# One transformer-and-scan block on one core: the output projection taken over two tiles of 128 positions, and the MLP products placed in the slots between

## The chip, the cores and the metric

The kernel runs on one core of a Trainium2 chip, which has a matrix engine (TensorE, PE in the rows, with PEld for its weight loads), a vector engine (VectorE, DVE), a scalar engine (ScalarE, ACT), a general engine (GpSimd, POOL) and a queue that issues transfers (SyncE, SP). Each engine works through its own list of instructions in order and waits on semaphores. The metric is the device time of one execution in microseconds (us); lower is better.

## The reference

The input x is 4 x 512 x 128 in f32. The block adds four parts to it, each on a layer-normalized input: gated linear attention, a feed-forward stage, a state-space (mamba) part, and the same feed-forward stage again:

```python
x = x + gla(layernorm(x))
x = x + ffn(layernorm(x))
x = x + mamba(layernorm(x))
x = x + ffn(layernorm(x))
```

Each feed-forward stage is itself six layers of local attention (16 heads of 64, windows of 32 that see themselves and the window before) and a gated MLP, all in f32:

```python
for i in range(6):
    h = shift_tokens(x)
    q, k, v = split(h @ Wqkv[i])                  # 128 -> 3 x 1024
    q, k = rotary(l2norm(q) * qs), rotary(l2norm(k) * ks)
    x = local_attention(q, k, v) @ Wo[i] + x      # 1024 -> 128
    h = shift_tokens(x)
    a, gate = split((norm(h) * g + b) @ W1[i] + b1)   # 128 -> 2 x 341
    x = (a * gelu(gate)) @ W2[i] + b2 + x             # 341 -> 128
```

## The kernel before

The change touches only the feed-forward stage, which runs twice. Its loop has one **iteration** `it` per layer and batch element (6 x 4 = 24 per stage) and in it four **slots** `u`, one per tile of 128 positions. The work is pipelined by hand: in slot u the engines finish the attention of tile u, make the scores of tile u+1 and project tiles u+2 and u+3. The MLP takes a whole batch element (512 positions, one instruction each) and runs one iteration behind: during iteration `it` the MLP of element `it - 1` is spread over the four slots (`mlp` in the code, false only in the first iteration). The order on each engine is written out in `pe_body`, `act_body` and `dve_body`, and semaphores hold it together; nothing is scheduled automatically.

A slot of PE goes: transposes of q (`pe_qk_t`, L279), chunk 2 of the q/k/v projection (`pe_proj`, L266 to L268, three matmuls each), the output projection of the tile before (`pe_wo`, L363), transposes of k, chunk 3, an MLP product, transposes of the probabilities (`pe_probs_t`, L294), the mask and half of the scores (L306, L313), chunk 4, in two slots an MLP product, the other half of the scores, chunk 5, a wait for the banks (`pe_pv_ready`, `pe_pv_banks`), chunk 0 of the next tile, P V (`pe_pv`, L328), and chunk 1. In this text a slot is counted from the start of P V in the rows (L328) to the next one, so that what stands above as first follows P V and one projection.

The MLP's steps: in slot 0 the centre product (`pe_center`, L369) and the variance (`pe_var`, L373); ACT takes a logarithm and an exponential of it (`act_rstd`, L534, L536, written to the tile `gelu`); DVE scales (`dve_norm`, L726, L729). Then three **up** products of 128, 128 and 85 columns, each for the gate (L385) and the value (L386), with the gelu on ACT (`act_gelu`, L547, behind a table load) and the product of the two on DVE (`dve_hidden`, L735). Then the **down** product (`pe_down`, L394) and its addition to the stream (`dve_down`, L742). Before the change the up products stand in slots 1, 2 and 2, the down product in slot 3.

The output projection, the MLP products and P V share two of PSUM's eight banks, `o_ps[0]` and `o_ps[1]`. ACT empties P V into `o_t` (`act_out_t`, L486); `pe_wo` reads it and writes 128 columns of `o_ps[0]`, which DVE adds to the stream (`dve_wo`, L719 and L720, 64 partitions each); only then may an MLP product or the next P V write the banks. V goes from ACT (`act_v`, L478) through 16 small transfers per tile, issued by SP, into `v_pairs`; ACT waits for those of the tile before. POOL adds the rotated halves (L860), scales by the norms (L870), normalizes the probabilities (L835) and, once per iteration, splits a weight (L849).

## Time and profile before

| | us |
|---|---|
| median of 3 runs | 3862.81 (3855.98 to 3873.53) |
| the profiled execution | 3830.92 |
| its span in the trace | 3829.1 |
| PE busy | 3454.3 |
| DVE, ACT, POOL busy | 3008.5, 2702.0, 2718.4 |
| output projection (L363) on PE, 3072 records | 387.9 |

The span is the time from the first to the last instruction of the trace; the profiled execution has 1.8 us around it. Each f32 matmul stands in the trace as two records, so eight matmuls are 16. Records overlap in the pipeline, so the time of a group is best read from its start to the start of what follows.

### The profile page before, as it was taken

How to read it: one execution, taken by the hardware profiler on the slowest of the kernel's cores; microseconds unless marked ns; L12 is line 12 of the kernel's file. 1: busy time of each engine (PE TensorE's matmuls, PEld its weight loads, DVE VectorE, ACT ScalarE, POOL GpSimd, SP SyncE). 2: the span in 40 equal slices, each digit the busy share in tenths (PEclk: the TensorE clock that was granted, in tenths of full speed). 3: DMA queues.
4: the chain of work that ended last, by engine and by line, in shares of the span. 5: the costliest groups of instructions: out<-in, count | busy, mean ns of one | idle time of the engine just before them, and what ended most of it. 6: DMA issues, size and time to landing. Idle time of an engine off the chain costs nothing. (4 is left out here: it accounts for less than half of the span.)

```text
span 3829.1 us, 153118 instructions
## 1 busy us (share of the span) xinstructions
PE 3454.3 (90%) x62588; PEld 2453.8 (64%) x62588; DVE 3008.5 (79%) x4752; ACT 2702.0 (71%) x7080; POOL 2718.4 (71%) x3091
## 2 busy tenths in 40 slices
PE   8799999999999999985555789999999999999996
PEld 3477777777777777762111267777777777777774
DVE  7688888878788788865888778888878888888884
ACT  2477778777878787763334468787777877787874
POOL 3588787777878787850334488787778787787872
PEclk9899999999999999996888899999999999999998
DMA  1233333333333333320000033233333333333331
GB/s 41 59 74 76 78 81 72 83 74 76 83 74 83 76 77 76 80 60 16 0 0 0 18 72 78 70 87 71 80 78 74 79 76 74 83 78 72 88 71 37
DMA packets 183102, 251.36 MB, mean 66 GB/s; under 512 B 53658, under 2 KB 74782, under 8 KB 182302
## 3 DMA queue, kind: packets, MB, share of 16 engines
q1 hardware_dynamic: 182422, 241.71, 26.5%
q8 instruction: 498, 8.16, 0.9%
q14 instruction: 182, 1.49, 0.1%
HBM read 39.13 MB, written 1.05 MB: 10 GB/s over the span
## 5 line engine op out<-in xcount | busy, mean ns | idle before, releaser
L860 POOL TENSOR_TENSOR qk_rows<-rot_products 128x512 f32<-128x512 f32 x768 | 982.4, 1281 | 213.1 <-DVE rot_products L659 212.2
L659 DVE TENSOR_TENSOR rot_products<-psum,rot_scaled 128x1024 f32<-128x1024 f32 x768 | 936.5, 1219 | 150.0 <-ACT squares L470 123.3
L870 POOL TENSOR_TENSOR qk_rows<-qk_rows,rnorm 128x512 f32<-128x512 f32 x768 | 804.0, 1078 | 15.0
L266 PE MATMUL psum<-wqkv_hi,xs_hi 128*128 128x512 f32 x1152 | 556.8, 483 | 81.3 <-DVE rot_products L659 42.4
L661 DVE TENSOR_REDUCE sumsq<-squares 128x8 f32<-128x512 f32 x768 | 518.6, 675 | 0.0
L470 ACT ACTIVATE squares<-psum 128x512 f32<-128x512 f32 x768 | 488.3, 636 | 41.6 <-PE psum L268 36.7
L478 ACT ACTIVATE v_rows<-psum 128x512 f32<-128x512 f32 x384 | 228.2, 595 | 358.1 <-DMA v_pairs<-v_rows 178.8
L835 POOL TENSOR_TENSOR probs<-probs,rden 128x512 f32<-128x512 f32 x384 | 392.5, 1043 | 103.7 <-DVE rden L709 102.7
L514 ACT ACTIVATE probs<-psum,minus_row_max 128x64 f32<-128x64 f32 x1536 | 457.2, 336 | 5.7 <-DVE minus_row_max L693 5.7
L267 PE MATMUL psum<-wqkv_lo,xs_hi 128*128 128x512 f32 x1152 | 457.3, 397 | 0.8 <-issue 0.8
L328 PEld LDWEIGHTS psum<-probs_t,v_pairs 64*64 64x64 f32 x24576 | 387.7, 135 | 109.5 <-issue 108.9
L268 PE MATMUL psum<-wqkv_hi,xs_lo 128*128 128x512 f32 x1152 | 457.7, 397 | 0.0
L328 PE MATMUL psum<-probs_t,v_pairs 64*64 64x32 f32 x24576 | 415.6, 220 | 33.8 <-issue 29.6
L363 PEld LDWEIGHTS psum<-o_t,wo 128*128 128x128 f32 x3072 | 362.0, 192 | 83.9 <-ACT o_t L486 63.1
L363 PE MATMUL psum<-o_t,wo 128*128 128x128 f32 x3072 | 387.9, 279 | 24.6 <-ACT o_t L486 17.2
L279 PE MATMUL psum<-ident,qk_rows 128*128 128x128 f32 x3072 | 401.4, 274 | 0.7 <-ACT q_t L497 0.7
L279 PEld LDWEIGHTS psum<-ident,qk_rows 128*128 128x128 f32 x3072 | 356.7, 142 | 28.1 <-issue 2.1
L1394 POOL TENSOR_TENSOR mb_hc<-mb_h,mb_c 128x512 f32<-128x512 f32 x128 | 159.7, 1268 | 293.9 <-DVE mb_h L1363 281.0
L313 PEld LDWEIGHTS psum<-k_t,q_t 64*32 64x32 f32 x24576 | 269.7, 105 | 152.3 <-issue 152.1
L514 ACT ACTIVATION_READ_ACCUMULATOR probs<-psum,minus_row_max 128x1 f32 x1536 | 354.2, 231 | 0.0
L266 PEld LDWEIGHTS psum<-wqkv_hi,xs_hi 128*128 128x128 f32 x1152 | 217.9, 189 | 179.8 <-issue 104.4
L313 PE MATMUL psum<-k_t,q_t 64*32 64x64 f32 x24576 | 332.2, 224 | 0.8 <-issue 0.8
(159 smaller groups left out, 6078.8 us busy)
## 6 DMA issues: line engine op xcount, KB each, us to landing
v_pairs<-v_rows SPq DMA_DIRECT2D x3072, 64.0 KB, 2.0
wqkv_staged<-in_Wqkv SPq DMA_DIRECT2D x52, 384.0 KB, 3.5
wo<-in_Wo SPq DMA_DIRECT2D x12, 512.0 KB, 4.7
w<-in_W SPq DMA_DIRECT2D x12, 341.0 KB, 3.4
qk_scale<-in_qk_scale SPq DMA_DIRECT2D x12, 128.0 KB, 3.4
w<-in_W SPq DMA_DIRECT2D x12, 128.0 KB
rot_base<-in_rot SPq DMA_DIRECT2D x2, 512.0 KB, 3.7
out_x<-qk_rows SPq DMA_DIRECT2D x1, 1024.0 KB, 5.1
```

Source lines behind the costliest of these rows:

```text
L266: nc.tensor.matmul(proj_ps[c % 2], xh, wh, start=True, stop=False)
L268: nc.tensor.matmul(proj_ps[c % 2], xl, wh, start=False, stop=True).then_inc(S["qkv_mm"], 1)
L279: last = nc.tensor.transpose(tr_ps[g % 2][:, i * P:(i + 1) * P], m["qk"][:, u % 2, (4 * g + i) * P:(4 * g + i + 1) * P], ident[:, :])
L313: last = nc.tensor.matmul(s_ps[par][WIN * w:WIN * w + WIN, 64 * hp:64 * hp + 64], m["qt"][rows, hp, WIN * w:WIN * w + WIN], m["kt"][rows, ...
L328: last = nc.tensor.matmul(o_ps[par][64 * j:64 * j + 64, P * (hp // 2) + WIN * w:P * (hp // 2) + WIN * w + WIN], m["vp"][rows, u % TILES, w ...
L363: last = nc.tensor.matmul(o_ps[0][:, 0:P], m["wo"][:, hp, :], m["ot"][:, hp, :], start=(hp == 0), stop=(hp == HP - 1))
L470: nc.scalar.activation(m["sq"][:, c % 2, :], proj_ps[c % 2], ACT.Square).then_inc(S["sq_done"], 1)
L514: last = nc.scalar.activation(m["p"][:, hp, 1, :], s_ps[1][:, 2 * WIN * hp:2 * WIN * (hp + 1)], ACT.Exp, bias=m["mx"][:, 1, hp:hp + 1], ac ...
L659: V.tensor_tensor(m["mm"][:, c % 2, :, :].rearrange("p a (h e) -> p a h e", e=DH), ps, cos_sin, ALU.mult)\
L661: V.tensor_reduce(m["ss"][:, HC * c:HC * c + HC], m["sq"][:, c % 2, :].rearrange("p (h e) -> p h e", e=DH), AX.X, ALU.add)\
L860: G.tensor_tensor(qk[:, c * CH:(c + 1) * CH].rearrange(half, a=2, e=DH // 2), cos, sin[:, :, ::-1, :], ALU.add)\
L870: G.tensor_tensor(part, part, m["rn"][:, u % 2, HC * c:HC * c + HC].unsqueeze(2) .to_broadcast([P, HC, DH]), ALU.mult).then_inc(S["rot_don ...
```

## The change

- `pe_wo` now takes half of the element's positions, two tiles, in one go: eight matmuls of 256 columns in place of two times eight of 128. It runs in slot 2 for tiles 0 and 1 and in slot 0 of the next iteration for tiles 2 and 3. `o_t` has room for two tiles, and DVE's addition covers 256 columns in the same two slots, behind the third of the four rotations.
- The up products 0 and 1 stand in slot 1, product 2 and the down product in slot 3. The first of each pair stands where the output projection stood, the second behind chunk 4.
- ACT's gelus and DVE's `hidden` follow; `dve_down` stands behind the norm's seed in slot 3. P V in slot 1 now waits for both of slot 1's `hidden` steps, in slot 2 for nothing of the MLP, in slot 3 as before for the stream.
- The normalized input overwrites the centred one (`ln_xc`), which saves a buffer.

The core of the diff:

```diff
-            m["ot"] = fsb("o_t", [P, HP, P])
-            m["xn"] = fsb("xn_mlp", [P, T])
+            m["ot"] = fsb("o_t", [P, HP, 2, P])
+            m["xn"] = ln_xc
...
             elif u == 1:
-                nc.tensor.wait_ge(S["h_done"], 2 * e + 1)
-            elif u == 2:
-                nc.tensor.wait_ge(S["hidden_done"], e + 1)
-            else:
+                nc.tensor.wait_ge(S["h_done"], 2 * (e + 1))
+            elif u == 3:
                 nc.tensor.wait_ge(S["stream"], B + e + 1)
...
-        def pe_wo(it, u):
...
+        def pe_wo(it, half):
+
+            if half == 0:
+                nc.tensor.wait_ge(S["wo_in"], (it // B + 1) * 16)
+            nc.tensor.wait_ge(S["oT_ev"], cnt(it, 2, 2 * half + 1, 2))
             for hp in range(HP):
-                last = nc.tensor.matmul(o_ps[0][:, 0:P], m["wo"][:, hp, :], m["ot"][:, hp, :],
+                last = nc.tensor.matmul(o_ps[0][:, 0:2 * P], m["wo"][:, hp, :],
+                                        m["ot"][:, hp, :, :].rearrange("p a q -> p (a q)"),
                                         start=(hp == 0), stop=(hp == HP - 1))
...
-                if prev:
-                    pe_wo(it, u - 1)
+                if mlp and u == 0:
+                    pe_wo(it - 1, 1)
+                if u == 2:
+                    pe_wo(it, 0)
+                if mlp and u == 1:
+                    pe_up(it - 1, 0, free)
+                if mlp and u == 3:
+                    pe_up(it - 1, 2, free)
...
-                if mlp and u in (1, 2):
-                    pe_up(it - 1, u - 1, added_)
-                if mlp and u == 3:
-                    pe_down(it - 1, added_)
                 pe_probs_t(it, u, nxt)
...
-                if mlp and u == 2:
-                    pe_up(it - 1, 2, added_)
+                if mlp and u == 1:
+                    pe_up(it - 1, 1, None)
+                if mlp and u == 3:
+                    pe_down(it - 1)
...
-                if mlp and u in (1, 2):
-                    act_gelu(it - 1, u - 1)
+                if mlp and u == 1:
+                    act_gelu(it - 1, 0)
+                if mlp and u == 3:
+                    act_gelu(it - 1, 2)
                 act_probs_t(it, u)
...
-                if mlp and u == 2:
-                    act_gelu(it - 1, 2)
-                if mlp and u in (1, 2):
+                if mlp and u == 1:
+                    act_gelu(it - 1, 1)
+                if mlp and u in (1, 3):
                     nc.scalar.preload_act_table_set("natural_log_exp_and_others")
...
-                if prev:
-                    dve_wo(it, u - 1)
                 if proj:
-                    dve_rotate(layer, j, u + 2, (2, 3))
+                    dve_rotate(layer, j, u + 2, (2,))
+                if mlp and u == 0:
+                    dve_wo(it - 1, 1)
+                if u == 2:
+                    dve_wo(it, 0)
+                if proj:
+                    dve_rotate(layer, j, u + 2, (3,))
                 if mlp and u == 1:
                     dve_hidden(it - 1, 0)
-                if mlp and u == 2:
+                if mlp and u == 3:
+                    dve_hidden(it - 1, 2)
+                if proj:
+                    dve_rnorm(it, u + 2)
+                if mlp and u == 1:
                     dve_hidden(it - 1, 1)
                 if mlp and u == 3:
                     dve_down(it - 1)
-                if proj:
-                    dve_rnorm(it, u + 2)
-                if mlp and u == 2:
-                    dve_hidden(it - 1, 2)
```

`free` is the count of `o_t` writes up to the slot before, so that an up product does not write the banks before ACT has emptied P V from them. The lines after the change are numbered by one to seven higher (L279 becomes L280, L328 L329, L363 L362, L735 L742).

PE in slot 1 before: the output projection (L363), transposes of k (L279), chunk 3, the first up product (L385, L386), transposes of the probabilities (L294), mask and first half of the scores.

```order
L363 MATMUL psum<-o_t,wo 128x128 x8
L279 MATMUL psum<-ident,qk_rows 128x128 x8
L266 MATMUL psum<-wqkv_hi,xs_hi 128x512
L267 MATMUL psum<-wqkv_lo,xs_hi 128x512
L268 MATMUL psum<-wqkv_hi,xs_lo 128x512
L385 MATMUL psum<-xn_mlp,w 128x512
L386 MATMUL psum<-xn_mlp,w 128x512
L294 MATMUL psum<-ident,probs 128x128 x8
L306 MATMUL psum<-maskrow,onehot 128x512 x2
L313 MATMUL psum<-k_t,q_t 32x64 x32
```

And after, from the second half of the first up product (L387) to the first of the second:

```order
L387 MATMUL psum<-ln_xc,w 128x512
L280 MATMUL psum<-ident,qk_rows 128x128 x8
L267 MATMUL psum<-wqkv_hi,xs_hi 128x512
L268 MATMUL psum<-wqkv_lo,xs_hi 128x512
L269 MATMUL psum<-wqkv_hi,xs_lo 128x512
L295 MATMUL psum<-ident,probs 128x128 x8
L307 MATMUL psum<-maskrow,onehot 128x512 x2
L314 MATMUL psum<-k_t,q_t 32x64 x32
L267 MATMUL psum<-wqkv_hi,xs_hi 128x512
L268 MATMUL psum<-wqkv_lo,xs_hi 128x512
L269 MATMUL psum<-wqkv_hi,xs_lo 128x512
L386 MATMUL psum<-ln_xc,w 128x512
```

The output projection is gone from the slot; between the first up product and the second stand two sets of transposes, chunk 3, half of the scores and chunk 4, where there was one product in the slot.

PE in slot 3 before, from the output projection to the transposed probabilities, with the down product (L394) between:

```order
L363 MATMUL psum<-o_t,wo 128x128 x8
L279 MATMUL psum<-ident,qk_rows 128x128 x8
L266 MATMUL psum<-wqkv_hi,xs_hi 128x512
L267 MATMUL psum<-wqkv_lo,xs_hi 128x512
L268 MATMUL psum<-wqkv_hi,xs_lo 128x512
L394 MATMUL psum<-hidden,w 128x512 x3
L294 MATMUL psum<-ident,probs 128x128 x8
```

And after, from the transposed probabilities (L295) to the second half of the scores (L314):

```order
L295 MATMUL psum<-ident,probs 128x128 x8
L307 MATMUL psum<-maskrow,onehot 128x512 x2
L314 MATMUL psum<-k_t,q_t 32x64 x32
L267 MATMUL psum<-wqkv_hi,xs_hi 128x512
L268 MATMUL psum<-wqkv_lo,xs_hi 128x512
L269 MATMUL psum<-wqkv_hi,xs_lo 128x512
L394 MATMUL psum<-hidden,w 128x512 x3
L314 MATMUL psum<-k_t,q_t 32x64 x32
```

The down product moved behind the transposed probabilities, half of the scores and chunk 4, and an up product stands where the output projection stood.

DVE in slot 2 before, from the second rotation (L659 with its sum L661) over the addition (L719, L720) to hidden 1 (L735):

```order
L659 TENSOR_TENSOR rot_products<-psum,rot_scaled 128x1024
L661 TENSOR_REDUCE sumsq<-squares 128x8
L719 TENSOR_TENSOR x_ffn<-psum,x_ffn 64x128
L720 TENSOR_TENSOR x_ffn<-psum,x_ffn 64x128
L659 TENSOR_TENSOR rot_products<-psum,rot_scaled 128x1024
L661 TENSOR_REDUCE sumsq<-squares 128x8
L659 TENSOR_TENSOR rot_products<-psum,rot_scaled 128x1024
L661 TENSOR_REDUCE sumsq<-squares 128x8
L735 SCALAR_TENSOR_TENSOR hidden<-psum,layer_vectors,gelu 128x512
```

And after, rotations (L665, L667), the addition (L726, L727) and the seed of the norms (L688):

```order
L665 TENSOR_TENSOR rot_products<-psum,rot_scaled 128x1024
L667 TENSOR_REDUCE sumsq<-squares 128x8
L665 TENSOR_TENSOR rot_products<-psum,rot_scaled 128x1024
L667 TENSOR_REDUCE sumsq<-squares 128x8
L726 TENSOR_TENSOR x_ffn<-psum,x_ffn 64x256
L727 TENSOR_TENSOR x_ffn<-psum,x_ffn 64x256
L665 TENSOR_TENSOR rot_products<-psum,rot_scaled 128x1024
L667 TENSOR_REDUCE sumsq<-squares 128x8
L688 TENSOR_SCALAR minus_sumsq<-sumsq 128x32
```

The addition covers 256 columns and stands one rotation later.

## Rows read from the trace of the kernel before

A few words recur: x16 behind a row is a count of records; "[0.71 <-ACT gelu L534]" is idle time before the row and what ended it.

**Rows 1.** The page: busy time of each engine, share of the span, instructions
```profile
PE 3454.3 (90%) x62588; PEld 2453.8 (64%) x62588; DVE 3008.5 (79%) x4752; ACT 2702.0 (71%) x7080; POOL 2718.4 (71%) x3091
```

**Rows 2.** Windows: feed-forward stage, then slots 0 to 3 (length, busy per engine, clock)
```profile
core 0: us, PE busy (x) PEld busy (x) DVE busy (x) ACT busy (x) POOL busy (x), PEclk, DMA share, GB/s
400.00:1600.00 1200.00, 1163.05 (x23530) 881.33 (x23523) 978.77 (x1605) 947.94 (x2571) 962.78 (x1117) 1.00 0.33 78
1330.60:1346.72 16.12, 15.30 (x321) 11.83 (x320) 13.20 (x22) 12.82 (x38) 13.44 (x17) 1.00 0.34 75
1346.72:1362.25 15.53, 15.02 (x321) 11.70 (x320) 13.63 (x23) 13.46 (x36) 13.88 (x16) 1.00 0.40 96
1362.25:1380.05 17.80, 17.33 (x325) 12.53 (x324) 12.74 (x23) 14.93 (x38) 14.66 (x19) 1.00 0.27 62
1380.05:1396.06 16.01, 15.92 (x323) 12.08 (x323) 13.25 (x23) 10.54 (x32) 10.36 (x13) 1.00 0.29 69
```

**Rows 3.** Timeline of PE, slots 0 to 2: start, length, operation, records, [idle before]
```profile
1335.36 1.95 PE L363 MATMUL psum<-o_t,wo 128*128 128x128 f32 x16
...
1337.14 1.04 PE L279 MATMUL psum<-ident,qk_rows 128*128 128x128 f32 x8
...
1345.86 0.47 PE L266 MATMUL psum<-wqkv_hi,xs_hi 128*128 128x512 f32 x1 [0.71 <-ACT gelu L534]
...
1351.76 2.02 PE L363 MATMUL psum<-o_t,wo 128*128 128x128 f32 x16 [0.52 <-ACT o_t L486]
...
1353.62 1.04 PE L279 MATMUL psum<-ident,qk_rows 128*128 128x128 f32 x8
...
1355.19 1.02 PE L385 MATMUL psum<-xn_mlp,w 128*128 128x512 f32 x2
...
1356.05 1.02 PE L386 MATMUL psum<-xn_mlp,w 128*128 128x512 f32 x2
...
1356.90 1.04 PE L294 MATMUL psum<-ident,probs 128*128 128x128 f32 x8
...
1359.87 0.86 PE L313 MATMUL psum<-k_t,q_t 64*32 64x64 f32 x64
...
1364.06 0.89 PE L328 MATMUL psum<-probs_t,v_pairs 64*64 64x32 f32 x44 [0.34 <-issue]
...
1375.49 1.02 PE L385 MATMUL psum<-xn_mlp,w 128*85 128x512 f32 x2
...
1379.19 0.47 PE L266 MATMUL psum<-wqkv_hi,xs_hi 128*128 128x512 f32 x1
```

**Rows 4.** Timeline of ACT, slots 0 and 1
```profile
1344.22 0.60 ACT L478 ACTIVATE v_rows<-psum 128x512 f32<-128x512 f32 x1 [2.38 <-DMA v_pairs<-v_rows]
...
1356.00 1.28 ACT L547 ACT_TABLE_LOAD   x1
```

**Rows 5.** Groups by form, DVE's addition of the output projection: busy, mean ns
```profile
L720 DVE TENSOR_TENSOR x_ffn<-psum,x_ffn 64x128 f32<-64x128 f32 x192 | 56.6, 295 | 2.6
```

**Rows 6.** Timeline of DVE, slots 0, 1 and 3
```profile
1346.19 1.30 DVE L726 SCALAR_TENSOR_TENSOR xn_mlp<-ln_xc,layer_vectors,gelu 128x512 f32<-128x512 f32 x1
...
1348.59 1.21 DVE L659 TENSOR_TENSOR rot_products<-psum,rot_scaled 128x1024 f32<-128x1024 f32 x1
...
1358.02 0.75 DVE L735 SCALAR_TENSOR_TENSOR hidden<-psum,layer_vectors,gelu 128x512 f32<-128x512 f32 x1
...
1390.94 1.51 DVE L742 SCALAR_TENSOR_TENSOR x_ffn<-psum,layer_vectors,x_ffn 64x512 f32<-64x512 f32 x2
```

**Rows 7.** Timeline of POOL, end of slot 0 and slot 1
```profile
1344.89 4.68 POOL L870 TENSOR_TENSOR qk_rows<-qk_rows,rnorm 128x512 f32<-128x512 f32 x4
...
1349.53 1.84 POOL L849 TENSOR_TENSOR wqkv_lo<-wqkv_staged,wqkv_hi 128x768 fp32r<-128x768 f32 x1
...
1351.33 1.27 POOL L860 TENSOR_TENSOR qk_rows<-rot_products 128x512 f32<-128x512 f32 x1
...
1352.56 2.04 POOL L835 TENSOR_TENSOR probs<-probs,rden 128x512 f32<-128x512 f32 x2
```

52 lines of the change are left out of this document (24 added, 28 removed).

## The prediction, made before the change was timed

> **What bounds the kernel now.** I read the page first, then the windows, then the timeline of each engine over one pass through the loop. In the page, TensorE (PE) is busy 90% of the span and the next engine 79% [rows 1]; the reader is to see that only PE can be the bound on average. In the stretch from 400 to 1600 us, which is pure feed-forward stage, PE is busy 1163 of 1200 us at the full clock (2.4 GHz) while DVE, ACT and POOL have about 20% idle each [rows 2]. One iteration (one batch element, four slots of one tile each) lasts 65.46 us: slots 0 to 3 take 16.12, 15.53, 17.80 and 16.01 us in the iteration that I walk through [rows 2]. Both stages together hold 46 iterations with an MLP in them (24 each, the first without), some 3010 us of the 3829. So what the change does is 46 times what it does to these four slots.
>
> Busy PE is not free-running PE. In slot 0 it stands still for 0.71 us before a projection until ACT has taken the logarithm, and ACT itself had stood 2.38 us until the transfers of V had landed, before it could empty V and turn to the logarithm [rows 3, 4]. In slot 1 PE arrives at the output projection 0.52 us before the o_t that it reads [rows 3]. Slot 3, in which PE is busy 15.92 of 16.01 us, leaves 16.0 - 1.78 (output projection) - 2.57 (down product, six records of 0.43) = 11.6 us at most for what all slots have in common. Four of these, four output projections (7.12), centre and variance (1.72), three up products (5.16) and the down product (2.57) are 63.0 us: of 65.46 at least 2.5 are waits. The loop is tight: whatever PE does earlier must find its input earlier.
>
> **Part 1, the output projection over two tiles.** Before, 16 records over 128 columns take 1337.14 - 1335.36 = 1.78 us, 0.111 each [rows 3]. The trace has no 256-column record. Upper bound: a 512-column record takes 0.43 us (1356.05 - 1355.19 = 0.86 for two) [rows 3], half of that is 0.214, and 16 of them 3.43 us. Lower bound: as little as 128 columns, 1.78 us. 0.111 stands close to a quarter of 0.43 (0.107), so records grow with their columns; I take 3.43. Per iteration that is 4 x 1.78 = 7.12 before and 2 x 3.43 = 6.86 after: 0.26 us less, 12 us over 46 iterations. On DVE the two additions of about 0.295 us each per slot become two over 256 columns in every second slot [rows 5]; between 0.295 at 128 columns and 0.75 at 512 (two in 1.51) [rows 6] I put one at 0.43 us. That frees 0.6 us of DVE per iteration, which has 20% to spare: nothing by itself.
> The Trainium skill (TensorE: Matmul & The Clock Gate, section "Back-to-back issue gap") has a sustained spacing of about 81 ns a matmul at 128 columns and 131 at 512, far less than in proportion. The trace disagrees: 0.111 against 0.43, nearly the full factor of four [rows 3]. By the page the wide product would be nearly half as long as I say; that is the fifth case below.
>
> **Part 2, slot 0.** The projection of the previous element's last two tiles stands here: 3.43 in place of 1.78, and behind it the transposes, the centre product and everything to the scores, all 1.65 us later. The centre product wants DVE's addition, which now stands behind a third rotation. PE comes to it 1337.14 - 1330.60 + 1.65 + 1.57 = 9.8 us into the slot [rows 3]; I take the addition as done by then, and 0.5 us, one addition, as the upper bound. The late V transfer is now covered: V is wanted 1.65 us later, the logarithm is done before the last projection, and the 0.71 us wait goes with its queueing, about 0.9 us. Slot 0: 16.12 + 1.65 - 0.95 = 16.8 us.
>
> **Part 3, slot 1: two MLP up products, no output projection.** Three things come late for PE.
> First the normalization. It ran on DVE from 1346.19 to 1348.59, ahead of the first rotation of slot 1, whose result PE's next projection wants [rows 6]. Now it starts 1.56 us later (behind scores that end 1.65 later), while the slot starts only 0.7 later. PE reaches that projection 3.6 us into the slot and its product is there at 4.1: 0.5 us of wait; up to 2 in the one iteration in four in which DVE also rescales its tables.
> Second POOL. Its four multiplications (4.68 us), the weight split (1.84), one addition (1.27) and the probabilities (2.04) run in one piece from 1344.89 to 1354.60 [rows 7], and all that is now 1.4 us later: probabilities at about 8.7 us into the slot. PE had come to their transposition 1356.90 - 1346.72 = 10.2 us into the slot [rows 3]; without an output projection it comes at 8.2. About 0.45 us of wait where there were 2.3 of slack.
> Third the chain of the MLP itself. The second up product writes the banks that the first product's gelu (ACT) and hidden (DVE) read. From the second half of the q/k transposes to the end of hidden it takes 1358.02 + 0.75 - 1353.62 = 5.15 us: ACT has two copies, a square, a table load of 1.28 and the gelu in the way, DVE the last rotation [rows 3, 4, 6]. PE needs from that same point 4.5 us to the place where the second product now stands (1355.19 - 1353.62 = 1.57 for the transposes and a projection, then 1356.90 to 1359.87 = 2.97) [rows 3]. So 0.7 us are short at the least; through POOL's lag, which holds the last rotation, it is 1.0 or a little more. In slot 2 before, the product between the two places gave 1.7 us more, which is why no such wait is seen there.
> A matmul that waits holds all that stands behind it on PE: half of the scores, a projection and P V. Behind the second product, gelu, hidden and the bank wait take 1379.19 - 1375.49 = 3.70 us, as they did in slot 2 [rows 3], then 0.86 to the next slot. Slot 1: second product at 4.4 + 0.5 + 1.7 + 4.5 + 0.45 + 1.0 = 12.55, and 3.7 + 0.86: 17.1 us against 15.53.
>
> **Part 4, slot 2** loses two up products (3.43) and gains 1.65: free-running that is 17.80 - 1.78 = 16.0; and the waits behind the second product (1379.19 stands 0.3 late) and of P V (0.34) [rows 3] are mostly gone, with 0.3 left for o_t: 15.1 us.
>
> **Part 5, slot 3: the last up product early, the down product behind the first half of the scores.** It loses 1.78 of output projection and gains 1.72 of up product: no change in free time. But the down product wants the last hidden. Its chain is again the 5.15 us, PE is there after 4.5: with the semaphore 0.75 to 0.9 us short. Before, the down product had a hidden from the slot before and no wait. And P V waits for DVE to add the down product (1.51 us) [rows 6], which was long over; now it starts 2.6 us after the product begins and PE has only 1.7 us of work meanwhile (half of the scores and a projection): 0.25 us. Slot 3: 16.01 + 1.0 = 17.0 us.
>
> **The sum.** 16.8 + 17.1 + 15.1 + 17.0 = 66.0 against 65.46: 0.54 us longer, 25 us over 46 iterations. The profiled execution took 3830.92 us and would take 3856; it is 32 us under the median of the runs, 3862.81, to which I add the same 25: 3888 us.
> The same number of table loads stands on ACT (two before gelus, two back per iteration); the output projection at each stage's end is 1.65 longer, 3 us in all, against first iterations that gain as much. The transfers of V take as long and are issued in the same order. The normalized input now overwrites the centred one; that waits only on products of the element before, over by then. These I put at zero, with 5 us either way.
>
> **Rivals.** A change of 0.5%, 19 us, is about what a measurement of this kernel can tell from none.
> Case 1, as summed: 3888, between 3870 and 3910. Chance 0.42.
> Case 2, waits only move: the 3.8 us of waits stay as large and only the free 0.26 us counts: 3850. For it: the slots hand their lateness on, and what PE waits for in one it does not wait for in the next; against it: two products now stand closer behind their inputs than before. 0.20.
> Case 3, the other side: slot 0's gain is whole (16.5 us) and POOL's lag doesn't reach PE, so that the MLP waits stay at their least, 0.7 in slots 1 and 3. Slots 16.5, 16.5, 14.9, 16.7 make 64.6, 0.86 less: 3823. It decides at POOL's probabilities: if they are ready 8.2 us into slot 1, no wait is added there. Against it: that run of POOL has no gap in it [rows 7]. 0.20.
> Case 4, lag on lag: the late normalization, POOL and, one iteration in four, the tables push the last rotation by 0.75 us more in slots 1 and 3 each and it isn't made good in slot 2: 67.5 us, +94 in all, or half of that: 3910 to 3957. 0.15.
> Case 5, a 256-column record costs little more than a 128-column one: up to 1.65 us less per pair, 3.3 per iteration: 3888 - 152 = 3736 at the lower bound. 0.03.
> Faster by over 0.5%: cases 3 and 5, 0.23. Within: case 2 and a fifth of case 1, 0.28. Slower: the rest, 0.49. The range of 8 in 10 goes from 3832 (most of case 2 and the near part of case 3) to 3935.
> That the change doesn't do what it says can be left out: the order of the instructions shows 8 matmuls of 256 columns per two tiles and the products where described.
>
> **What would show it.** L362's records 0.214 apart. Slot 0 near 16.8 us with no idle time for the logarithm before its last projection; in slot 1 idle time before the second up product (0.7 to 1.1 us) put down to DVE's hidden, and some before the transposed probabilities put down to POOL; slot 2 near 15 us; in slot 3 0.8 us before the down product. I am wrong if the iteration comes out under 65 us, or if the longer waits stand elsewhere, above all before the centre product or for V's transfers.

## The result, and the profile after

The changed kernel takes 3953.05 us (median of four runs, 3943.11 to 3953.73) against 3864.4 us of the kernel before on the same chip: ratio 1.0223, 95% interval 1.0194 to 1.0252. It is slower by 2.2%, about 89 us. I had predicted 3888 and a range up to 3935, so the direction was right and the size was not: the time fell into my fourth case ("lag on lag", 67.5 us per iteration, 3910 to 3957), which I had given 0.15. The profiled execution took 3943.11 us (3830.92 before), 112 us more, of which 23.5 are only that the execution profiled before stood 33.5 us under its median and this one 10 under. Executions at a lower granted clock are left out of all ratios; there was one, of e8 below (4328 us at a clock of 0.73, where its others have 0.96).

The page's line of each engine, the feed-forward stage, and slots 0 to 3 of one iteration, which answer to [rows 1, 2]:

```profile
PE 3487.2 (88%) x61052; PEld 2382.9 (60%) x61052; DVE 3001.4 (76%) x4560; ACT 2703.5 (69%) x7080; POOL 2715.1 (69%) x3091
```
```profile
core 0: us, PE busy (x) PEld busy (x) DVE busy (x) ACT busy (x) POOL busy (x), PEclk, DMA share, GB/s
400.00:1600.00 1200.00, 1137.94 (x22324) 824.32 (x22323) 949.34 (x1490) 920.37 (x2489) 933.55 (x1084) 1.00 0.32 76
1025.79:1042.60 16.81, 16.72 (x321) 12.91 (x321) 12.70 (x21) 13.18 (x37) 10.45 (x14) 1.00 0.40 97
1042.60:1059.76 17.16, 15.72 (x310) 10.65 (x309) 14.28 (x23) 14.56 (x37) 15.61 (x17) 1.00 0.36 86
1059.76:1075.60 15.84, 15.23 (x317) 12.23 (x317) 12.68 (x21) 10.44 (x32) 10.65 (x15) 1.00 0.30 69
1075.60:1093.17 17.57, 16.53 (x312) 10.74 (x311) 13.09 (x21) 13.59 (x36) 15.55 (x19) 1.00 0.27 63
```
Every engine is less busy in the stage than before, PE too (1138 of 1200 us against 1163), at the same clock. So no work was added: waits were. (Per iteration PE is busy 0.6 us more than before, 0.948 of 67.48 us against 0.969 of 65.43; the products and their columns are the same, and the balance below, from start to start, shows no longer work in it.) Most sit in slots 1 and 3, where PE is idle 1.44 and 1.04 us; in slot 0 PE is busy 16.72 of 16.81 us.

**The balance.** A feed-forward iteration can be cut out of the trace 44 times with nothing missing, from P V's first record to P V's first record four slots on. Means of those, and what PE would need if each step took its shortest record of the trace (a common slot is 11.15 us: P V 2.00, six pieces of projection 4.70, transposes and scores 4.45; narrow output projection 1.78, wide 3.45, up product 1.72, down 2.58, centre and variance 1.81):

| us | slot 0 | slot 1 | slot 2 | slot 3 | iteration |
|---|---|---|---|---|---|
| before | 15.94 | 15.84 | 17.53 | 16.13 | 65.43 |
| of it waits | 1.20 | 1.19 | 1.16 | 0.62 | 4.2 |
| after | 16.90 | 17.38 | 15.54 | 17.66 | 67.48 |
| of it waits | 0.49 | 2.79 | 0.94 | 2.21 | 6.4 |
| my walk | 16.8 | 17.1 | 15.1 | 17.0 | 66.0 |

The free part fell by 0.22 us (predicted 0.26), and waits rose by 2.3. Over all 46 iterations, with those at a phase's end, the means are 65.18 and 67.30: 98 of the 112 us. The other 14 are the ends of the stages: the first iteration starts 1.8 us later, the piece between the two stages is 5.8 and the tail 7.0 us longer.

**Slots 1 and 3 on PE**, which answer to [rows 3]:

```profile
1030.40 3.72 PE L362 MATMUL psum<-o_t,wo 128*128 128x256 f32 x16
1033.96 1.04 PE L280 MATMUL psum<-ident,qk_rows 128*128 128x128 f32 x8
...
1051.27 1.09 PE L295 MATMUL psum<-ident,probs 128*128 128x128 f32 x8 [0.23 <-POOL probs L846]
...
1055.08 1.13 PE L386 MATMUL psum<-ln_xc,w 128*128 128x512 f32 x2 [0.72 <-DVE hidden L742]
...
1064.46 3.69 PE L362 MATMUL psum<-o_t,wo 128*128 128x256 f32 x16 [0.18 <-ACT o_t L490]
...
1073.81 0.27 PE L314 MATMUL psum<-k_t,q_t 64*32 64x64 f32 x2 [0.44 <-issue]
...
1087.53 2.82 PE L394 MATMUL psum<-hidden,w 128*128 128x512 f32 x6 [0.63 <-DVE hidden L742]
...
1092.31 0.47 PE L267 MATMUL psum<-wqkv_hi,xs_hi 128*128 128x512 f32 x1 [0.28 <-issue]
```
The wide product takes 3.56 us with its queueing, the second up product and the down product each wait for hidden, and behind the down product a projection has 0.28 us of idle time ahead of it, at the place of the wait for the addition. In the means the step that ends at the second up product is 0.85 us over its shortest, the product itself 0.19, the last two pieces 0.48: 1.5 us for the second product in slot 1, and by the same count 1.5 in slot 3. Before, the one such place, in slot 2, cost 0.5. That alone is 2.5 us more than before: this is where the time of the changed kernel stands. It does not say what would give it back; the experiments do.

**Why hidden is late**, on DVE, POOL and ACT [rows 4, 6, 7]:

```profile
1036.36 1.23 DVE L665 TENSOR_TENSOR rot_products<-psum,rot_scaled 128x1024 f32<-128x1024 f32 x1 [1.19 <-ACT squares L474]
...
1052.55 1.23 DVE L665 TENSOR_TENSOR rot_products<-psum,rot_scaled 128x1024 f32<-128x1024 f32 x1 [1.24 <-POOL qk_rows L871]
...
1054.29 0.74 DVE L742 SCALAR_TENSOR_TENSOR hidden<-psum,layer_vectors,gelu 128x512 f32<-128x512 f32 x1
```
```profile
1037.67 1.29 POOL L871 TENSOR_TENSOR qk_rows<-rot_products 128x512 f32<-128x512 f32 x1 [2.28 <-DVE rot_products L665]
...
1041.50 4.68 POOL L881 TENSOR_TENSOR qk_rows<-qk_rows,rnorm 128x512 f32<-128x512 f32 x4
...
1051.17 1.27 POOL L871 TENSOR_TENSOR qk_rows<-rot_products 128x512 f32<-128x512 f32 x1
```
```profile
1052.99 0.69 ACT L551 ACTIVATE gelu<-psum,layer_vectors 128x512 f32<-128x512 f32 x1
```
Read it backwards. Hidden (1054.29) follows DVE's last rotation (1052.55), which had waited 1.24 us for POOL's addition. POOL had run in one piece since 1041.50, and there it had started late after 2.28 us of idle time. What it idled for is DVE's last rotation of slot 0 (1036.36), and that had waited for the fourth piece of projection, which stands behind the wide product. The wide product in slot 0 thus costs something in slot 1. The gelu ended at 1053.68, only 0.6 us before hidden began: a second chain, nearly as late. In the means of slot 1 the last rotation ends 11.28 us in, the gelu 11.27, hidden begins at 11.82 and the second product at 12.62.

The view of waits, 400 to 1600 us (in total, times, longest), of before:
```profile
POOL qk_rows L860 <- DVE rot_products L659: 75.4, 138, 1.8
...
ACT v_rows L478 <- DMA v_pairs<-v_rows: 60.5, 31, 3.4
...
PE psum L266 <- ACT gelu L534: 9.7, 9, 1.6
...
DVE rot_products L659 <- POOL qk_rows L860: 3.0, 6, 0.6
```
and of after:
```profile
POOL qk_rows L871 <- DVE rot_products L665: 111.4, 68, 2.4
...
DVE rot_products L665 <- POOL qk_rows L871: 23.4, 25, 1.2
...
PEld psum L386 <- DVE hidden L742: 20.0, 18, 1.2
...
PEld psum L295 <- POOL probs L846: 13.1, 22, 0.8
...
PE psum L394 <- DVE hidden L742: 12.3, 18, 0.8
```
PE's wait for the logarithm is gone, and each of the 18 iterations in the window now has both waits for hidden.

### The profile page after: what moved, and what is told of

It is laid out like the page before. It is cut to its first block and busy times, and to the rows that moved or that the text cites. A ratio compares the mean times of both kernels' runs of the same rounds, so it can differ in the third digit from the quotient of the medians.

```text
span 3941.3 us, 149848 instructions
## 1 busy us (share of the span) xinstructions
PE 3487.2 (88%) x61052; PEld 2382.9 (60%) x61052; DVE 3001.4 (76%) x4560; ACT 2703.5 (69%) x7080; POOL 2715.1 (69%) x3091
## 5 line engine op out<-in xcount | busy, mean ns | idle before, releaser
L665 DVE TENSOR_TENSOR rot_products<-psum,rot_scaled 128x1024 f32<-128x1024 f32 x768 | 935.7, 1218 | 289.2 <-ACT squares L474 205.8
L667 DVE TENSOR_REDUCE sumsq<-squares 128x8 f32<-128x512 f32 x768 | 518.9, 676 | 0.0
L329 PEld LDWEIGHTS psum<-probs_t,v_pairs 64*64 64x64 f32 x24576 | 383.8, 135 | 100.8 <-issue 100.3
L329 PE MATMUL psum<-probs_t,v_pairs 64*64 64x32 f32 x24576 | 409.5, 220 | 27.7 <-issue 24.0
L280 PEld LDWEIGHTS psum<-ident,qk_rows 128*128 128x128 f32 x3072 | 362.5, 142 | 94.0 <-issue 54.7
L280 PE MATMUL psum<-ident,qk_rows 128*128 128x128 f32 x3072 | 403.3, 275 | 5.6 <-ACT q_t L501 5.4
L501 ACT ACTIVATE k_t<-psum 128x512 f32<-128x512 f32 x384 | 208.8, 596 | 285.1 <-PE psum L280 285.1
L314 PEld LDWEIGHTS psum<-k_t,q_t 64*32 64x32 f32 x24576 | 270.4, 105 | 181.7 <-issue 181.4
L362 PE MATMUL psum<-o_t,wo 128*128 128x256 f32 x1536 | 361.6, 390 | 17.7 <-ACT o_t L490 14.5
L314 PE MATMUL psum<-k_t,q_t 64*32 64x64 f32 x24576 | 335.1, 224 | 13.0 <-issue 12.9
L362 PEld LDWEIGHTS psum<-o_t,wo 128*128 128x128 f32 x1536 | 290.2, 193 | 89.5 <-issue 28.0
```

What stands on the lines that cost most here:

```text
L280: last = nc.tensor.transpose(tr_ps[g % 2][:, i * P:(i + 1) * P], m["qk"][:, u % 2, (4 * g + i) * P:(4 * g + i + 1) * P], ident[:, :])
L314: last = nc.tensor.matmul(s_ps[par][WIN * w:WIN * w + WIN, 64 * hp:64 * hp + 64], m["qt"][rows, hp, WIN * w:WIN * w + WIN], m["kt"][rows, ...
L329: last = nc.tensor.matmul(o_ps[par][64 * j:64 * j + 64, P * (hp // 2) + WIN * w:P * (hp // 2) + WIN * w + WIN], m["vp"][rows, u % TILES, w ...
L362: last = nc.tensor.matmul(o_ps[0][:, 0:2 * P], m["wo"][:, hp, :], m["ot"][:, hp, :, :].rearrange("p a q -> p (a q)"), start=(hp == 0), sto ...
L665: V.tensor_tensor(m["mm"][:, c % 2, :, :].rearrange("p a (h e) -> p a h e", e=DH), ps, cos_sin, ALU.mult)\
L667: V.tensor_reduce(m["ss"][:, HC * c:HC * c + HC], m["sq"][:, c % 2, :].rearrange("p (h e) -> p h e", e=DH), AX.X, ALU.add)\
```

## The experiments

Ratios are to the kernel before on the same chip, intervals 95%. Slots and iterations are means over the same 44 iterations of each profile.

| kernel | ratio | slots 0 to 3 | iteration |
|---|---|---|---|
| before | 1 | 15.94 15.84 17.53 16.13 | 65.43 |
| changed | 1.0223 | 16.90 17.38 15.54 17.66 | 67.48 |
| e1 wide only | 1.0168 | 16.85 15.38 19.56 15.48 | 67.27 |
| e2 spread only | 1.0294 | 15.83 18.00 15.24 19.04 | 68.11 |
| e3 changed, no tables | 1.0191 | 17.01 17.36 15.45 17.52 | 67.34 |
| e4 before, no tables | 0.9985 | 16.08 15.99 17.51 16.14 | 65.72 |
| e5 wide cut in two | 1.0263 | 18.07 17.10 15.29 17.38 | 67.84 |
| e6 e5, no tables | 1.0208 | 18.00 17.00 15.24 17.06 | 67.30 |
| e7 changed, 10 transfers | 1.0193 | 16.93 17.31 15.39 17.60 | 67.23 |
| e8 before, 10 transfers | 0.9842 | 15.17 15.84 17.30 16.09 | 64.40 |
| e10 last up product in slot 2 | 1.0512 | 17.65 17.37 18.01 16.43 | 69.45 |
| e11 e10, 10 transfers | 1.0403 | 17.88 17.31 17.51 16.23 | 68.93 |
| e12 e5, centre later | 1.0248 | 17.69 17.02 15.30 17.40 | 67.42 |
| e13 e10, addition earlier | 1.0233 | 17.10 17.39 18.04 15.18 | 67.71 |
| e14 e8, norm later | 0.9854 | 15.17 16.14 17.26 16.07 | 64.65 |

**e1 and e2: each half of the change alone.** The changed kernel with the MLP products at their old places (e1):
```diff
-                if mlp and u == 1:
-                    pe_up(it - 1, 0, free)
-                if mlp and u == 3:
-                    pe_up(it - 1, 2, free)
...
+                if mlp and u == 1:
+                    pe_up(it - 1, 0, free)
+                if mlp and u == 2:
+                    pe_up(it - 1, 1, None, it * HALVES + 1)
+                if mlp and u == 3:
+                    pe_down(it - 1, free)
                 pe_probs_t(it, u, nxt)
```
and the kernel before with the MLP products in their new slots, each behind the narrow output projection (e2; ACT and DVE follow):
```diff
-                if mlp and u in (1, 2):
+                if mlp and u in (1, 3):
                     pe_up(it - 1, u - 1, added_)
-                if mlp and u == 3:
-                    pe_down(it - 1, added_)
...
-                if mlp and u == 2:
-                    pe_up(it - 1, 2, added_)
+                if mlp and u == 1:
+                    pe_up(it - 1, 1, added_)
+                if mlp and u == 3:
+                    pe_down(it - 1, added_)
```

> The changed kernel with the wide output projection (slots 0 and 2), but the MLP products back where they stood before the change (up 0 in slot 1, up 1 and 2 in slot 2, down in slot 3, each behind chunk 3 or 4). My theory: the loss comes from the second MLP product of slots 1 and 3 waiting for gelu and hidden of the first, and from P V behind them; here those waits are gone, free time on PE is 0.26 us per iteration less than before, so an iteration takes 65.0 to 65.6 us (65.2 before, 67.3 after in the profiles) and the time is within 1% of the kernel before. Rival A: the wide projection costs by itself (longer records, DVE's addition behind the third rotation, POOL's lag in slot 1): then the iteration stays above 66.5 us and the time 1.5 to 2% above before.

> The kernel before (128-column output projection in every slot), with the MLP products placed as the change places them: up 0 and up 1 in slot 1, up 2 and down in slot 3, the second of each behind chunk 4; the first behind chunk 3 as before. My theory: between the first and the second product there is as much work as in slot 2 of the kernel before, so no wait for hidden; only P V in slot 3 now waits about 0.3 us for the addition of the down product: iteration 65.2 to 65.7 us, time within 0.7% of before. Rival B: that two products in slots 1 and 3 are bad in themselves (table load in slot 3, late hidden, the addition behind the seed): iteration over 66.3, time 1.5% or more over before.

Measured: 1.0168 [1.0131, 1.0205] and 1.0294 [1.0252, 1.0336]. My theory, that each part costs little by itself, fell, and both rivals held: each part alone costs 1.5% or more. Alone they add 1.84 and 2.68 us per iteration, together 2.05 and not 4.5: each covers a part of the other's cost. e1 shows a wait that I had not foreseen:
```profile
PE psum L280 <- ACT q_t L507: 34.6, 32, 1.4
```
In slots 1 and 3, with neither output projection nor product between the two halves of the transposes, PE reaches the second half before ACT has copied o_t and q_t: in the means the step ahead of it is 0.91 and 1.17 us over its shortest, against 0.22 and 0.21 before. The narrow output projection had been the cover for these copies, so taking 1.78 us out of slots 1 and 3 returned 0.46 and 0.65. In e2 it is V:
```profile
ACT v_rows L476 <- DMA v_pairs<-v_rows: 104.5, 39, 4.3
...
PE psum L266 <- ACT v_rows L476: 24.6, 18, 2.1
```
The transfers of slot 1's tile begin 0.5 us into slot 2, as before the change (0.4), and their 16 issues take 11.4 us (means), with 2.0 us from issue to landing. Slot 2, now without an MLP product, is too short for them: PE wants the next bank 12.9 us in, and ACT, which waits for the landing, has emptied it at 14.2. PE waits 1.4 us.

**e3 and e4: no table loads**, in the changed kernel and in the one before. Both leave out the gelu and keep its bias (in the kernel before the load stands at `u in (1, 2)`):
```diff
-                if mlp and u in (1, 3):
-                    nc.scalar.preload_act_table_set("natural_log_exp_and_others")
...
-ACT.Gelu,
+ACT.Identity,
```

> The changed kernel with the gelu replaced by an addition of the bias alone (Identity, no table loads in the loop; the MLP's gate isn't the reference's). It takes 1.28 us out of the chain from the first product to hidden. My theory: idle time of 0.68 us before the second up product and before the down product goes, and slot 1 and slot 3 get 0.7 to 1.1 us shorter each; the iteration takes 65.3 to 66.0 us against 67.3. Rival C: ACT isn't on the path there (POOL's lag holds the last rotation and so hidden): then slots 1 and 3 shrink by less than 0.4 us each.

> The same in the kernel before, as a control (bias alone in place of the gelu, no table loads). My theory: only slot 2 has a wait on that chain (hidden before P V, 0.3 us) and the V transfers start up to 1.3 us earlier after slots 1 and 2: iteration 0.3 to 0.8 us shorter, 64.4 to 64.9. Rival C: it gains as much as the changed kernel does.

Measured: 1.0191 [1.0143, 1.0239] and 0.9985 [0.9963, 1.0007]. Rival C held: slots 1 and 3 change by 0.02 and 0.14 us. The gelus of the first products end 1.4 and 1.5 us sooner, the last rotation in slots 1 and 3 ends where it did (11.3 and 10.6 us in), and the second products still stand 12.6 and 12.0 us in. So ACT's chain is not what holds them alone. (e4's mean has one iteration of 72.58 us in it; the medians of the 44 are 65.29 before and 65.25 in e4.)

**e5, e6, e12: the wide product cut in two**, heads 4 to 7 behind the fourth piece. With it the centre product moves behind the transposed probabilities (slot 0), and DVE's addition behind the last rotation (slots 0 and 2):
```diff
                 if mlp and u == 0:
-                    pe_wo(it - 1, 1)
+                    pe_wo(it - 1, 1, range(4))
...
                 if mlp and u == 0:
+                    pe_wo(it - 1, 1, range(4, HP))
+                if u == 2:
+                    pe_wo(it, 0, range(4, HP))
+                pe_probs_t(it, u, nxt)
+                if mlp and u == 0:
                     pe_center(it - 1)
-                pe_probs_t(it, u, nxt)
...
+                if proj:
+                    dve_rotate(layer, j, u + 2, (3,))
                 if mlp and u == 0:
                     dve_wo(it - 1, 1)
                 if u == 2:
                     dve_wo(it, 0)
-                if proj:
-                    dve_rotate(layer, j, u + 2, (3,))
```

(e5; e6 adds the edit of e3; e12 puts `pe_center` behind `pe_scores(it, u + 1, 0)`.)

> The changed kernel with one thing different: the wide output projection of slots 0 and 2 is cut in its list of eight heads. Heads 0 to 3 stay ahead of the last q/k transposes, heads 4 to 7 follow the fourth piece of the projection. The centre product and the addition to x move behind it. Same products, same columns. THEORY (chain over POOL): the whole wide product stands ahead of the fourth piece, which comes 1.65 us late; DVE's last rotation, POOL's norm multiplications and so POOL's probabilities and second addition of the next slot (1 and 3) follow 1.4 late, and PE waits there. With the split the fourth piece comes 1.7 us earlier in slots 0 and 2, POOL has no 2.3 us of idle time before its norm multiplications there, and the last rotation of slots 1 and 3 is no longer held by POOL. The wait for the probabilities in slot 1 (0.35 us) goes; of the 0.8 us before each second product only 0.1 to 0.3 goes, since the gelu chain on ACT ends almost as late. Iteration 66.4 to 67.0 us instead of 67.48: ratio to the kernel before 1.008 to 1.016. RIVAL (the wide product is what costs, wherever it stands): iteration 67.4 or more, ratio 1.02 to 1.025, with the waits at other places. SECOND RIVAL (waits of slots 1 and 3 come from POOL's work in that slot alone): POOL's idle time in slots 0 and 2 goes, the last rotation of slots 1 and 3 stays as late, ratio 1.02.

> The same split of the wide projection, and in addition the gelu is replaced by a copy with bias, with no table loads (the gelu is left out of what is computed). THEORY (two chains end together before the second product: POOL to the last rotation to hidden, and ACT's tables to gelu to hidden): the loads alone, taken from the changed kernel, gave 0.14 us per iteration; with both taken away the stall before the second products falls from 0.8 to 0.3 us or less in slots 1 and 3, and the iteration is 65.7 to 66.3 us, ratio 0.998 to 1.006. RIVAL (POOL's lag does not come from the place of the wide product): as the changed kernel without table loads, iteration 67.3, ratio 1.019.

> The split wide projection of the earlier run, with the centre product behind the first half of the scores instead of directly behind the transposed probabilities, where it had waited 0.77 us for the addition to x. THEORY: slots 1 to 3 stay at what the split gave them (17.1, 15.3, 17.4), and slot 0 loses the wait for the addition but takes one before the variance product, since two copies on ACT (1.2 us) now stand against one piece of projection (0.8): slot 0 17.2 to 17.6 us, iteration 67.0 to 67.4, ratio about 1.018. RIVAL (the gain in slots 1 to 3 came only because slot 0 was longer and gave POOL and ACT time): slots 1 to 3 return to 17.4, 15.5, 17.7 while slot 0 falls, iteration 67.5 or more.

Measured: 1.0263 [1.0231, 1.0295], 1.0208 [1.0166, 1.0249], 1.0248 [1.0198, 1.0298]: all three slower than I expected, e5 and e12 no faster than the changed kernel and e6 no faster than e3. Slots 1 to 3 of e5 are as expected: the wait for the probabilities is gone (1.15 to 0.78 us for the step), DVE's waits for POOL, 23.4 us in the changed kernel, don't appear among e5's, and slots 1 to 3 are 0.81 us shorter. In slot 0 my edit lost 1.17, in a place that I had not priced (1.0 of it at this place): the centre product waits for the addition, which now comes after the second half.
```profile
PE psum L371 <- DVE x_ffn L733: 12.7, 18, 0.7
```
e12 moved the centre product, slot 0 fell by 0.38, and slots 1 to 3 stayed (17.02, 15.30, 17.40). Slot 0 is still 0.79 longer than in the changed kernel, so for slot 1 this speaks against the rival (the gain is a gift of slot 0's length) without settling it. Slot 3's gain, 0.26 to 0.28, is clear of it: the slot ahead of it, slot 2, got the cut too and is shorter, not longer. e6's iteration (67.30) is the number of its rival, but not its mechanism: against e3 slots 1 to 3 gain 1.03 us and slot 0 loses 0.99. The wait before the second up product over its shortest step: 0.85 in the changed kernel, 0.82 without tables, 0.76 with the cut, 0.48 with both. Neither chain alone is worth 0.1 us, both together 0.37: two chains that end together. What is left in e6 stands on DVE: in slot 1 the gelu ends 10.12 us in, the last rotation 10.81, and hidden begins, behind that rotation's sum, at 11.32.

**e7 and e8: 10 transfers for V's windows instead of 16**, the same bytes:
```diff
-                for half in range(2):
-                    for w in range(WPT):
...
+                for w in range(1, WPT):
+                    SP.dma_start(m["vp"][64 * par:64 * par + 2 * WIN, t, w, :],
+                                 m["v"][WIN * (w - 1):WIN * (w + 1), u % 2, par, :]).then_inc(vp_sem[t], 16)
```

> The changed kernel with the V windows of a tile moved by 10 transfers instead of 16 (windows that lie behind each other within the tile go in one transfer; the same bytes). THEORY: in the changed kernel the 16 issues take 10.9 us of each 16.5, and V of slot 1's tile, which is late behind the gelu, makes ACT late in slot 2; its excess over my walk (15.54 against 15.1) comes from there. With 10 transfers issue to landing falls from 13.3 to about 9 us, ACT's 1.9 us idle before V goes, slot 2 comes to 15.1 and the other slots stay: iteration 66.9 to 67.1, ratio 1.015 to 1.018. The waits before the second products stay at 0.8. RIVAL (V's transfers are what makes the changed kernel slower altogether): ratio 1.00 to 1.005, with all stalls gone. RIVAL 2 (transfers are covered, nothing changes): 1.022.

> The kernel before with the V windows of a tile moved by 10 transfers instead of 16, the same bytes. THEORY: in it V's landing makes ACT stand 2.4 us in slot 0, and PE 0.7 us before the last projection for the logarithm. With 10 transfers this goes: 0.6 to 0.9 us per iteration, ratio 0.989 to 0.994, iteration 64.6 to 64.9 us instead of 65.43. RIVAL (the lateness goes on to the next wait, on POOL or DVE): within 0.3%, ratio 0.997 to 1.0. RIVAL 2: longer transfers take as long as more short ones, ratio 1.0 with ACT's wait for V unchanged.

Measured: 1.0193 [1.0161, 1.0226] and 0.9842 [0.9802, 0.9882]. SP's issues for one tile, in the kernel before and in e8 (first and last of six rows):
```profile
1330.63 10.76 SPq L916 DMA_DIRECT2D v_pairs<-v_rows  x16
```
```profile
797.41 0.54 SPq L910 DMA_DIRECT2D v_pairs<-v_rows  x1
...
802.28 2.57 SPq L915 DMA_DIRECT2D v_pairs<-v_rows  x3
```
10.8 us have become 7.4 (medians of all 192 tiles: 11.2 and 7.2). In the kernel before ACT's wait for the transfers is gone from the list of waits, slot 0 falls by 0.77, and the kernel is 1.6% faster, more than theory and rivals gave it. In the changed kernel the same edit gives 0.25 us: slot 0's wide product already covered most of the transfers. With them out of the way the change costs 2.83 us per iteration, not 2.05.

**e10, e11, e13: the last up product in slot 2**, the down product early in slot 3, so that only slot 1 has two products (e11 adds the 10 transfers):
```diff
                 if mlp and u == 3:
-                    pe_up(it - 1, 2, free)
+                    pe_down(it - 1, free)
...
-                if mlp and u == 3:
-                    pe_down(it - 1)
+                if mlp and u == 2:
+                    pe_up(it - 1, 2, None, it * HALVES + 1)
```

> The changed kernel with the last up product moved from slot 3 to slot 2, behind its fifth piece of projection, and the down product moved to the place in slot 3 that the up product had. Wide output projections, columns and table loads as in the changed kernel; only slot 1 now holds two MLP products. THEORY (what costs is a slot in which two MLP products share the banks: the second waits for the gelu and hidden of the first, and P V for what follows the second): slot 3 loses its up product (1.74), the wait before the down product (0.87), its slower start (0.17) and the wait of P V (0.37) and comes to 14.5 us; slot 2 gains 1.81 and 0.4 of waits behind it and comes to 17.7; slots 0 and 1 stay at 16.9 and 17.4. Iteration 66.3 to 66.7 us, ratio to the kernel before 1.006 to 1.012. RIVAL A (waits go on to the next place: the slots hand on their lateness): iteration 67.3 to 67.6, ratio 1.02 to 1.026. RIVAL B (slot 3's wait is POOL's lag from the wide product of slot 2, so the up product in slot 2 only adds): slot 3 keeps 0.5 us or more of waits before its scores, ratio 1.015 or more.

> The same placement, and V's windows moved by 10 transfers instead of 16. THEORY: the two gains are separate; 0.25 us per iteration off the former, as in the changed kernel, or up to 0.5 if V had become late in slots 2 and 3: ratio 1.000 to 1.008. It stays 1.5 to 2.5% behind the kernel before with 10 transfers, since the wide projection gives only 0.26 per iteration and slot 1 keeps its waits. RIVAL (with this placement V's transfers are what binds): 1 us off or more, ratio under 0.998.

Measured: 1.0512 [1.0466, 1.0559] and 1.0403 [1.0351, 1.0454]. Both are far behind their theories. The wait before the down product went, and a worse one came. Rows of DVE and PE in slot 3 of e11:
```profile
836.49 1.51 DVE L755 SCALAR_TENSOR_TENSOR x_ffn<-psum,layer_vectors,x_ffn 64x512 f32<-64x512 f32 x2
```
```profile
838.31 0.47 PE L267 MATMUL psum<-wqkv_hi,xs_hi 128*128 128x512 f32 x1 [1.39 <-ACT v_rows L488]
```
The profile puts PE's 1.39 us down to ACT's copy of V, but that had ended at 837.56. PE's queue stands there at the waits of P V, one of which is for the addition that ends at 838.00. I had left the addition behind rotation and norm. e13 is e10 with it ahead of the last rotation:
```diff
+                if mlp and u == 3:
+                    dve_down(it - 1)
                 if proj:
                     dve_rotate(layer, j, u + 2, (3,))
```

> The placement with the last up product in slot 2 and the down product early in slot 3, with one correction: DVE's addition of the down product stands ahead of the last rotation of slot 3 instead of behind rotation and norm. In the earlier run P V of slot 3 and the projection ahead of it waited 1.4 to 2.4 us for that addition, which ended 14.9 us into the slot. THEORY (a slot with two MLP products pays for the second, a slot with one does not): the addition is done 9 us into slot 3, slot 3 comes to 14.5 to 14.9, slot 0 back to 17.0, slot 2 stays at 17.5 to 18.0, slot 1 at 17.4: iteration 66.5 to 67.2, ratio to the kernel before 1.010 to 1.020, 0.5 to 1 us per iteration under the changed kernel. RIVAL (lateness goes on: V's transfers for slot 3, late behind the gelu of slot 2, or POOL, hold slot 3 to 16 us all the same): iteration 68.5 or more, ratio 1.035 or more. Then the earlier run's cost was not the addition.

Measured: 1.0233 [1.0209, 1.0256]. That lies between theory and rival. Slot 3 fell to 15.18 and slots 0 and 1 are as expected, yet the iteration is 67.71, no better than the changed kernel's: slot 3 gave back 2.48 us and slot 2 took 2.50, 1.72 of work and 0.78 of waits. With 10 transfers (e11) slot 2 is 0.5 shorter, so a part of these is V's. My theory of the price of a second product holds for one slot at a time, and not for the sum.

**e14: e8 with the normalization behind slot 1's first rotation:**
```diff
                     dve_rotate(layer, j, u + 2, (0,))
+                if mlp and u == 1:
+                    dve_norm(it - 1)
...
-                if mlp and u == 0:
-                    dve_norm(it - 1)
```

> The kernel before with 10 V transfers, and DVE's two normalization instructions moved from ahead of the first rotation of slot 1 to behind it. The narrow placement has its first up product 8.8 us into slot 1, so that the normalization has time; PE's third piece of projection there waited 0.86 us for the rotation. THEORY: that wait goes; slot 1 falls from 15.84 to 15.0 to 15.4 us, iteration 63.6 to 64.0, ratio to the kernel before 0.972 to 0.979. RIVAL (POOL's probabilities of slot 1 take its place: they end 8.8 us into the slot and PE would want them at 9.2): ratio 0.980 to 0.985, as with 10 transfers alone.

Measured: 0.9854 [0.9831, 0.9876]: no gain over e8. The wait that the rows name (0.86 us) is gone, and 1.16 us of others stand behind it in the same slot (third and fourth piece 0.65, second transposes 0.42, the up product 0.07, the output projection 0.02). The rival was right in its number and not in its place: the transposed probabilities, for which it had PE wait, begin with no more than that 0.07 ahead of them.

## Why the prediction was wrong

**The step that failed is the sum, "66.0 against 65.46".** My walk through the four slots gave what a changed iteration takes when nothing comes late by chance. Its fastest repeated value in the trace is 66.53 (eight of the 46 iterations, within 0.02): 16.81, 17.15, 15.14, 17.43 against my 16.8, 17.1, 15.1, 17.0. The 65.46 that I subtracted was of another kind: the iteration that I walked through held a 0.71 us wait for the logarithm, 0.52 for o_t and a 0.34 us gap in P V [rows 3], and is by luck within 0.03 of the mean of all such iterations, chance waits included.

Against that mean I would have needed the changed kernel's mean, 67.48. So of the 1.51 us between my +0.54 and the +2.05 of the means, 0.95 is waits of the changed kernel that come and go (67.48 - 66.53), for which my sum has no term, 0.53 is my walk on an iteration without them, 0.43 of it slot 3, and 0.03 the reference. Setting the fastest against the fastest gives the same lesson: full iterations of the kernel before reach 64.23 and 64.25 (these two only, the next is 64.45), so the change is +2.29, and the medians say +2.33 (65.27 and 67.60).

The waits that come and go are mostly gaps in P V (0.72 us over the four slots) and in the second scores of slot 2 (0.29). The kernel before has them too (0.94 in P V): they are not what the change added, but my 65.46 held 1.02 us of them and my 66.0 no more than the 0.39 of slot 0. Slot 1 of every fourth iteration, with DVE's tables, takes 17.79 us against 17.20 to 17.35 in the others; I had named that wait and left it out of the sum.

**Part 1** held: 16 records of 256 columns take 3.45 us and 3.55 in the mean (predicted 3.43), the two additions 0.41 and 0.43 (predicted 0.43):
```profile
L362 PE MATMUL psum<-o_t,wo 128*128 128x256 f32 x560 | 129.7, 385 | 5.2 <-ACT o_t L490 3.8
L726 DVE TENSOR_TENSOR x_ffn<-psum,x_ffn 64x256 f32<-64x256 f32 x35 | 14.2, 406 | 0.0
L727 DVE TENSOR_TENSOR x_ffn<-psum,x_ffn 64x256 f32<-64x256 f32 x35 | 15.0, 429 | 0.5
```
(385 ns is a record with its queueing; 3.45 / 16 = 0.216 apart.) The Trainium skill's spacing of 81 ns at 128 and 131 at 512 columns (TensorE: Matmul & The Clock Gate, "Back-to-back issue gap"), by which I had made case 5, is not what this trace shows: its 216 ns a record at 256 columns is already over the page's figure for 512.

**Part 2** held in its mechanism (no wait for the logarithm, none for the centre) and, partly by luck, in its level, 16.8: P V of the slot that I walked through took 2.39 us where 2.00 is usual, and a clean changed slot has 0.25 us ahead of the wide product and 0.11 in it instead. Its price was not +0.68 but +0.96, since slot 0 takes 15.94 in the mean and not 16.12.

**Part 3** held: second up product at 12.6 (predicted 12.55), 0.60 us for the normalization (0.5), 0.38 for the probabilities (0.45), 0.85 before the second product (1.0). Behind its start come 4.76 us, and I had 4.56.

**Part 4** met its level, 15.14 in the clean iterations, by luck: the terms that it names, 16.0 less 0.3 and 0.34, give 15.4 at the least. The slot that I walked through held more than I named, 0.63 us in P V and 0.12 in the scores. It was also subtracted from 17.80 where the mean is 17.53, and 0.4 of waits came on top in the mean: 0.29 is the gap in the second scores, and 10 transfers (e7) take 0.15 us from the slot.

**Part 5** was 0.43 short on the clean iteration. The down product takes 0.17 more than before, the two pieces of projection behind it 0.42 (predicted 0.25), and the one ahead of the up product 0.09. The wait before the down product, 0.87, was inside my 0.75 to 0.9.

**Stage ends** I put at zero (3 us of longer product against first iterations that gain as much), and they are 14: the first iteration starts 1.8 us later and gains nothing. Of the 5.8 us between the stages and the 7.0 of the tail, 4.6 and 7.2 stand between the start of the last P V and the centre product, where the wide product meets PE after idle time. Before, the window over the last output projection:
```profile
3788.00:3790.40 2.40, 2.05 (x16) 1.86 (x16) 0.00 (x1) 0.26 (x1) 0.00 (x0) 1.00 0.00 0
```
and after, its timeline rows, the window, and the same product at the end of the first stage:
```profile
3893.82 1.08 PE L329 MATMUL psum<-probs_t,v_pairs 64*64 64x32 f32 x32 [1.60 <-issue]
...
3896.11 6.37 PE L362 MATMUL psum<-o_t,wo 128*128 128x256 f32 x16 [1.22 <-ACT o_t L490]
...
1773.41 6.18 PE L362 MATMUL psum<-o_t,wo 128*128 128x256 f32 x16 [1.21 <-ACT o_t L490]
```
```profile
3896.00:3902.50 6.50, 6.37 (x16) 4.86 (x16) 0.00 (x0) 0.06 (x1) 0.00 (x0) 0.58 0.00 0
```
The granted clock is 0.58, near the lower of its two levels (1.2 GHz), where before it was 1.00, and 16 records took 6.37 us where 3.72 is the length of such a row in the loop. Of the 4.3 us (6.37 - 2.05) 1.7 are the wider product at the full clock and 2.6 the clock; another 2.6 are P V, which has 1.60 us of idle time between its records. The kernel before has such a stretch in its tail too, one tile earlier, behind idle times of 1.33 and 1.40 us, and there the down product pays, with 5.09 us where such a row takes 2.74 in the loop:
```profile
3778.23 5.09 PE L394 MATMUL psum<-hidden,w 128*128 128x512 f32 x6 [0.68 <-DVE x_ffn L720]
```
```profile
3775.00:3780.00 5.00, 4.32 (x18) 3.09 (x18) 0.58 (x2) 0.00 (x0) 1.90 (x2) 0.60 0.00 0
```
At the end of the first stage it has none (1.00 from 1700 to 1722 us), where the changed kernel's clock is 0.50 from 1773 to 1776. That the idle time brings the lower clock is what both kernels' rows suggest; no run here tests it.

**The cases.** Case 4 has the right size by luck. It is true that lag goes from one slot into the next (e5 undoes 0.81 us of it in slots 1 to 3), but case 4 had it as 0.75 us more before each second product, and there the waits are 0.85 and 0.87, those of case 1. Case 3 assumed that POOL's lag doesn't reach PE; it does (0.38 us and the rotation). Case 2, waits only move, is what happens among placements (e13), but not from before to after.

**What stays open:** why P V and the scores have gaps that no releaser explains (0.44 us before the scores' last records in slot 2, 0.35 in P V, here and in the kernel before). With 10 transfers the gaps in P V of the kernel before shrink from 0.94 to 0.46 us per iteration, so V's transfers have a part in them, by what way is not shown. The other 1.2 of the 5.8 us between the stages are open too. Nor did any run with the wide product come below a ratio of 1.0168: that some placement of it would is neither shown nor excluded.

## What to carry to other kernels

Subtract like from like: a walk that assumes no chance waits is compared with the kernel's cleanest iterations, or the chance waits, taken from the means of many iterations, are added to it as a term of their own. Work between two dependent steps is a cover; the 1.78 us taken from slots 1 and 3 returned a third, because ACT's copies then stood bare. And when one stretch is made longer to relieve another, follow the longest chain out of it into the next slot: here PE, square, rotation, POOL, rotation, hidden, PE.

## What the runs showed that I had not expected

The largest lever was elsewhere: 16 against 10 transfers of the same bytes is worth 1.6% in the kernel before and 0.25 us an iteration (0.4%) in the changed one. All table loads taken away give 0.14 us in the changed kernel and nothing that can be told in the one before (ratio 0.9985 [0.9963, 1.0007]). And in the tail of both kernels a stretch at a granted clock near 0.6 follows idle times of 1.2 to 1.7 us on PE: which product happens to stand in it, the down product before, the wide one after, takes 1.7 to 1.9 times as long.
